# MLP down products one run later in two scan layers, and one chunk of the scan input made by another engine

## The reference

```python
def step(hst, ins):                       # one direction, over time
    dt_t, B_t, C_t, x_t = ins
    dA = jnp.exp(dt_t[:, :, None] * A)
    hst = hst * dA + (dt_t * x_t)[:, :, None] * B_t[:, None, :]
    return hst, jnp.einsum('bds,bs->bd', hst, C_t)
...
x = x + gate * (h_fwd + h_bwd)            # both directions' scans
h, gate = _adaln(x, c, adaln_mlp_w, adaln_mlp_b)
mlp_out = jax.nn.silu(h @ mlp_w1) * (h @ mlp_w2) @ mlp_w3
return x + gate * mlp_out
```

## Time and profile before

| | us |
|---|---|
| median of 3 runs | 4444.14 |
| lowest, highest | 4440.59, 4447.8 |
| the profiled execution | 4434.66 |
| its span, first to last instruction | 4432.9 |

### The profile page before, as it was taken

One profiled execution on the slowest core, in us unless ns is written; L12 is line 12 of the kernel. 1 busy time (PEld: TensorE's weight loads), 2 busy tenths in 40 slices (PEclk: granted clock), 3 DMA queues, 4 the chain that ended last, 5 costly groups with the idle time before them and its releaser, 6 DMA issues.

```text
span 4432.9 us, 109964 instructions
## 1 busy us (share of the span) xinstructions
PE 4148.3 (94%) x45790; PEld 3230.5 (73%) x45790; DVE 4007.4 (90%) x3859; ACT 3865.3 (87%) x6050; POOL 3623.7 (82%) x1328
## 2 busy tenths in 40 slices
PE   9999899899899988999989999999999999999998
PEld 6457677677677764458877777778777778777777
DVE  6669999999999976659999999999999999999996
ACT  4569899899899964569999999999999999999995
POOL 3339898798889973349999998999998999988995
PEclk9999999999999999999999999999999999999999
DMA  4012122121122221032242422422422423323221
GB/s 168 1 29 68 58 66 66 53 59 67 57 60 67 65 78 41 1 44 82 86 80 83 87 67 77 83 77 82 83 76 74 81 83 94 66 81 67 76 79 40
DMA packets 241501, 305.18 MB, mean 69 GB/s; under 512 B 116449, under 2 KB 175713, under 8 KB 241009
## 3 DMA queue, kind: packets, MB, share of 16 engines
q1 hardware_dynamic: 241008, 298.15, 24.5%
HBM read 289.84 MB, written 8.26 MB: 67 GB/s over the span
## 4 chain that ended last, share of the span: by engine, by line
PE 39%; ACT 37%; DVE 15%; issue 7%; POOL 1%; DVEq 0%; DMA 0%; SPq 0%; POOLq 0%; ACTq 0%
ACT weights_c L1800 10%; PE psum L863 9%; DVE work L2316 8%; PE psum L1152 8%; PE psum L1134 7%; ACT work L1817 7%; PE psum L1131 7%; ACT work L1800 7%; PE psum L1279 5%; ACT weights_c L1817 5%; DVE weights_c L2316 4%; ACT L1498 2%; ACT modulation L1800 2%; PE psum L1362 1%; PE psum L1075 1%
## 5 line engine op out<-in xcount | busy, mean ns | idle before, releaser
L2739 POOL TENSOR_TENSOR work<-work,weights_a 128x2048 f32<-128x2048 f32 x512 | 1977.0, 3872 | 139.9 <-DVE work L2316 106.6
L2316 DVE TENSOR_TENSOR_SCAN work<-weights_c,psum 128x512 f32<-128x512 f32 x1316 | 1509.0, 1203 | 81.0 <-PE psum L1134 69.3
L2739 POOL TENSOR_TENSOR weights_c<-weights_c,weights_a 128x2048 f32<-128x2048 f32 x256 | 989.4, 3873 | 50.2 <-DVE weights_c L2316 49.6
L1134 PE MATMUL psum<-ident,work 128*128 128x128 f32 x5464 | 932.6, 273 | 0.0
L1800 ACT ACTIVATE work<-work,decay 128x504 f32<-128x504 f32 x1172 | 817.8, 709 | 53.4 <-DVE weights_c L2316 27.4
L1134 PE MATMUL psum<-ident,weights_c 128*128 128x128 f32 x3752 | 694.5, 275 | 0.0
L2316 DVE TENSOR_TENSOR_SCAN work<-work,psum 128x512 f32<-128x512 f32 x586 | 675.2, 1201 | 20.1 <-PE psum L1134 16.9
L2316 DVE TENSOR_TENSOR_SCAN weights_c<-work,psum 128x512 f32<-128x512 f32 x586 | 675.7, 1201 | 19.1 <-PE psum L1134 18.5
L1152 PE MATMUL psum<-ident,work 64*128 64x64 f32 x16800 | 659.0, 229 | 10.6 <-POOL work L2739 7.6
L1134 PEld LDWEIGHTS psum<-ident,work 128*128 128x128 f32 x5464 | 668.2, 142 | 0.0
L1152 PEld LDWEIGHTS psum<-ident,work 64*128 64x128 f32 x16800 | 586.7, 140 | 99.8 <-issue 75.4
(11 more groups left out here) (221 smaller groups left out, 6453.9 us busy)
## 6 DMA issues: line engine op xcount, KB each, us to landing
weights_a<-c_rows SPq DMA_DIRECT2D x384, 512.0 KB, 3.7
work<-b_diagonals SPq DMA_DIRECT2D x240, 128.0 KB, 2.2
weights_c<-b_diagonals SPq DMA_DIRECT2D x112, 128.0 KB, 2.1
b_diagonals<-weights_c SPq DMA_DIRECT2D x1, 4096.0 KB, 18.1
weights_c<-in_L_cond_fwd_in_w SPq DMA_DIRECT2D x8, 512.0 KB, 5.2
weights_c<-in_L_cond_fwd_xproj_w SPq DMA_DIRECT2D x4, 1024.0 KB, 7.3
weights_c<-in_L_cond_bwd_in_w SPq DMA_DIRECT2D x8, 512.0 KB, 5.4
weights_c<-in_L_cond_bwd_xproj_w SPq DMA_DIRECT2D x4, 1024.0 KB, 7.5
```

Source lines behind the costliest of these rows:

```text
L1134: last = nc.tensor.transpose(PS[:, bank, t * P:(t + 1) * P], buf["scaled"][s % INPUTS][t][:, j * P:(j + 1) * P], IDENT[:, :])
L2316: v.tensor_tensor_scan(buf["ring"][s % RING][:, along, j], buf["decay"][q % DECAYS[l]][:, along], PS[:, 4 + q % LOOKAHEAD, along], 0.0, AL ...
L2739: g.tensor_tensor(state, state, row.unsqueeze(2).broadcast_to([P, T, DC]), ALU.mult).then_inc(ss["prod_ready"], 1)
```

## The change

It does four things.

1. Layer 3: down0 goes from runs 2, 4, 6 to the head of runs 3, 5, 7, ahead of down1. With it out of the list, the other jobs of runs 2, 4, 6 are spread wider: "dt" ends at step 205, "bc" stands at 208 to 216, "bt" at 220. In runs 3, 5, 7 down0 is at steps 3 to 11, down1 at 15 to 23, and what follows is later: the turns of "ytb" at 27 to 39 instead of 15 to 27, "in" at 115 to 139 instead of 108 to 133.
2. Layer 1: both downs of runs 3 and 5 go to runs 4 and 6, ahead of "ytb": down0 at step 3, down1 at 7 to 9. Those of run 7 and of the last block stay. The gated values (GLU1) get other memory, and the MLP norm of runs 4 and 6 waits for down1.
3. Runs 2, 4, 6 of layer 3: in every third state (`fourth_by_pool`) GpSimd scales the fourth chunk too, and TensorE turns it, where it made the diagonal product: 64 states in all, 256 products become transposes. The diagonals are still loaded.
4. In the same runs half of the thirds that were GpSimd's are ScalarE's: 32 ACTIVATEs more there, 32 operations fewer on GpSimd, which has 64 fourths more.

```diff
+def downs1(r):
+    return r // 2 - 2 if r in (4, 6) else r // 2 - 1 if r in (RUNS - 1, RUNS) else None
...
-def third_by_pool(s):
-    return s % INPUTS == 1
+def crowded(l, s):
+    return l == 3 and closes(s // PIPES[3].states)
+def third_by_pool(l, s):
+    return s % INPUTS == 1 and not (crowded(l, s) and s % (2 * INPUTS) == 1)
+def fourth_by_pool(l, s):
+    return crowded(l, s) and s % INPUTS == 0
...
     if r >= 3 and r % 2:
-        jobs += [("down1", DC, 3)]
+        jobs += [(f"down{c}", DC, 3) for c in range(KC)]
...
-    if closes(r):
-        jobs += [("down0", DC, 5)]
...
+    if tail and head and downs1(r) is not None:
+        jobs += [("down0", HIDDEN1, 3), ("down1", HIDDEN1, 3)]
     if tail:
         jobs += [(f"ytb{j}", 1, 3) for j in range(DC)] + [(f"out{c}", DC, 3) for c in range(KC)]
...
-    if gated:
+    if gated and downs1(r) is not None:
         jobs += [("down0", HIDDEN1, 3), ("down1", HIDDEN1, 8)]
...
-PIPES = {1: Pipe(32, 2, pipe_jobs1, 1, lambda r: 2 if r % 2 else 12 if r >= 2 else -IN_GAP),
+PIPES = {1: Pipe(32, 2, pipe_jobs1, 1, lambda r: 2 if r % 2 or r in (4, 6) else 12 if r >= 2 else -IN_GAP),
...
-        GLU1 = lambda r: region(WORK, 9216, HIDDEN1, T) if r < RUNS else region(WC, 13824, HIDDEN1, T)
+        GLU1 = lambda r: [A3.rearrange("p d j n -> p (d j n)"), region(SPENT, 0, T), H1B[:, 0, :]] if r < RUNS else [
+            region(WC, 13824 + T * k, T) for k in range(HIDDEN1)]
...
-            scaled=[[region(WORK, 11264 + o, DI) for o in (0, 512, 1024)],
+            scaled=[[region(WORK, 11264 + o, DI) for o in (0, 512, 1024)] + [region(SPENT, T, DI)],
...
-                    nc.tensor.matmul(PS[:, bank, SCALED * P:T], buf["dtx"][r % 2][:, SCALED, j * P:(j + 1) * P],
-                                     buf["diagonal"][:, s // 2 % 2, s % 2, :], start=True, stop=True)
-                    for t in range(SCALED):
+                    if j == 0 and fourth_by_pool(l, s):
+                        pe.wait_ge(ss["fourth_ready"], len([k for k in range(s + 1) if fourth_by_pool(l, k)]))
+                    if not fourth_by_pool(l, s):
+                        nc.tensor.matmul(PS[:, bank, SCALED * P:T], buf["dtx"][r % 2][:, SCALED, j * P:(j + 1) * P],
+                                         buf["diagonal"][:, s // 2 % 2, s % 2, :], start=True, stop=True)
+                    for t in range(TT if fourth_by_pool(l, s) else SCALED):
...
-                    loaded = n >= 2 * MADE_HERE
-                    mine_here = SCALED - 1 if third_by_pool(s) else SCALED
+                    loaded = n >= 2 * MADE_HERE or fourth_by_pool(l, s)
+                    mine_here = SCALED - 1 if third_by_pool(l, s) else SCALED
...
                     if ends:
-                        yield from tail(r, plan, bank, done, YT1(r), Z1, f"silu_z@{r - 2}", nb)
+                        yield from tail(r, plan, bank, done, YT1(r), Z1, f"silu_z@{r - 2}", nb,
+                                        close(downs1(r)) if head and downs1(r) is not None else ())
...
-                        yield from norm(r, plan, done, 3, H1B, nb, f"up2@{r - 1}" if r >= 4 else None)
+                        yield from norm(r, plan, done, 3, H1B, nb, f"down1@{r if head else r - 1}" if r >= 4 else None)
...
+                def chunks(s):
+                    if third_by_pool(l, s):
+                        chunk(s, 2, "third_ready")
+                    if fourth_by_pool(l, s):
+                        chunk(s, SCALED, "fourth_ready")
```

67 lines of the change are left out of this document (34 added, 33 removed).

## The result

The changed kernel takes 4452.75 us (median of 20 runs, 4447.55 to 4460.56), the kernel before in the same session 4443.97 (20 runs, 4436.18 to 4450.37). The ratio is 1.0023, 95% interval [1.0018, 1.0029]: the change makes the kernel 8.8 us **slower**. 4433 was forecast, and 4446 was the end of the range. The profiled execution took 4450.12 us with a span of 4448.1.

A forecast was written before the change was run, and what follows sets the result against it. The scan on VectorE was taken as the floor, with VectorE's idle time in crowded runs to win. The terms -8.5 + 1.0 - 4.5 + 1.0 = -11 against 4444.1 gave 4433 us, range 4417 to 4446.

The forecast's parts named there:

- Part 3: Layer 1, downs of runs 3 and 5 moved to runs 4 and 6: +1.0 us, bounds -5 and +7.
- They enter the head of run 4: Layer 1, receiving head: 2.4 us of VectorE work plus 1.5 of new idle, +3.9 a run.
- They leave a stretch where TensorE is busy 46.9 of 47.2: Layer 1, runs losing the downs: 2.4 us of VectorE work plus 1.0 of idle saved, -3.4 a run.
- The point that I had set for the forecast to be wrong: Layer 1, head of run 4: forecast wrong if it takes over 6 us more; other failure signs concerned layer 3.
- Part 1, the stall: Layer 3, runs 2, 4, 6: less VectorE idle around TensorE's "bc" wait, -8.5 us, bounds 0 and -12.
- no TensorE wait of over 2 us: Expected sign in layer 3: TensorE waits no more than 2 us for ScalarE's "bc" copy.
- no half clock behind it: Expected sign in layer 3: TensorE does not run at the lower clock after the "bc" wait.
- Part 1, the receiving runs: Layer 3, runs 3, 5, 7: down0's VectorE work of 1.2 us a run plus 0.3 a run, the latter booked as +1.0.
- Part 2: Layer 3, runs 2, 4, 6: transposes for diagonal products, half the thirds by ScalarE, -4.5 us, bounds 0 and -16.5.
- ScalarE's thirds: Rival: ScalarE, with 6.5 us more, bounds layer 3's runs 2, 4, 6; total -4, 4440 us; chance 0.26.
- the relief: Rival: TensorE's relief in layer 3's runs 2, 4, 6 pays in full; total -22, 4422 us; chance 0.17.
- GpSimd is no bound: Rival denied here: GpSimd becomes the bound in layer 3's runs 2, 4, 6; +22, 4466 us; chance 0.10.

The follow-up runs named there:

- e3: Kernel before with only layer 3's down0 one run later; chunks and layer 1 as before: 4434.17 us, ratio 0.9988.
- e2: Changed kernel with layer 1 put back as before, so only the layer 3 changes (down0 move and chunks): 4434.62 us, ratio 0.9986.
- e13: Layer 3 as e10, other jobs of runs 3, 5, 7 at old steps; layer 1 downs moved, residual first, other jobs at old steps, turns earlier: 4427.06 us.
- run 5: Not a follow-up kernel: a numbered stretch of a scan layer within one execution; before the change 302.2 us in layer 3, 185.7 us in layer 1.
- e4: Kernel before with only the chunk changes in layer 3's runs 2, 4, 6; down products and layer 1 as before: 4433.37 us, ratio 0.9983.
- e8: Changed kernel, layer 1: down0's VectorE operations ahead of the copies, other jobs at old steps, downs one product a step: 4436.59 us, ratio 0.9991.
- e6: Changed kernel, layer 1's runs 3 to 6: other jobs at the steps of before, downs one product a step: 4445.42 us, ratio 1.0012.
- e10: e2 with all thirds left to GpSimd, none given to ScalarE: 4428.98 us, ratio 0.9971.
- e12: e2 with down1 starting two steps later in layer 3's runs 3, 5, 7: 4433.74 us, ratio 0.9982.
- e15: Layer 3 as e10; layer 1's downs stay in runs 3 and 5, only turns bt, dtx0, dtx1 earlier: 4429.29 us, ratio 0.9955.

## Why the prediction was wrong

**Part 3: this step failed.** "They enter the head of run 4 ... I put 1.5 of new idle on it: +3.9 a run" measured +7.4 and +8.0. The mechanism was named correctly, with its place: the sums are copied only after scan 9, down0's residual stands behind them, TensorE wants the bank at step 7. Its price was not: VectorE was idle 4.0 us in the head for 0.9 before in run 4 and 0.0 in run 6, so 3.1 and 4.0 of new idle time for the 1.5 that I put there. I had priced TensorE's pause (4.6 forecast, 3.0 measured) and not what stands around it: three products due at one step, and two products at the lower clock level. And I looked no further than the head: the downs ahead of "ytb", with a start ten steps earlier, moved out0, out1 and mean by up to two steps and cost 2.1 more. "They leave a stretch where TensorE is busy 46.9 of 47.2 ... -3.4 a run" measured -1.0 and -1.8. There the freed time went to a wait that already existed behind it, 1.70 us, and grew to 3.23, and to a plan spread by 0.655 instead of 0.635 that put 20 product records into steps 64 to 79 where 16 were. My bounds for part 3 ended at +7; it cost 12.6. The point that I had set for the forecast to be wrong, a head over 6 us longer, was all but reached in run 4 (5.8) and passed in run 6 (6.9).

**Part 1, the stall: the number near, the mechanism not.** I took 8.5 us off for TensorE's wait for the "bc" copy, and with the moved 3.5 that is -12; the three MLP runs fell by 12.8 with down0 alone (e3). But only 3.0 of them stand from step 208 on, no more than down0's own operations, and VectorE is idle there 12.3 us for 12.6 (15.1 in the changed kernel). The idle time left steps 208 to 223 and came back in steps 224 to 255. The other 9.8 us come from steps 0 to 207, where I had booked nothing for down0's move but a mention that the work gets thinner. That the two nearly cancel is luck. The signs that I set say the same: "no TensorE wait of over 2 us" and "no half clock behind it" failed, with 2.12 us in run 4, 2.32 in run 6 and a granted clock of 0.91 and 0.89 in steps 224 to 239 of these runs.

**Part 1, the receiving runs: mis-sized.** Charged were 1.2 us of work and 0.3 more a run, 4.5 in all; measured 8.3 (e3), 8.7 (e2), 11.0 (the changed kernel). Of e3's 8.3 us, 7.2 stand ahead of step 208, where the jobs closer together cost more than the two operations: steps 80 to 111 of the three runs alone take 3.6 more. With the other jobs at their old steps (e13) these stretches are as before, and the cost stands in the first 32 steps. The last 16 steps differ by 2 us with the clock for the same code (run 5: 22.4 and 20.4 for 18.9).

**Part 2: the sum right, of two terms that I had not put so high.** -4.5 was forecast; e4 shows -4.3 over runs 2 to 7 in the profile and -7.5 by the ratio, [-12, -3]. It is 10.7 us won ahead of step 208, 5.8 of them in the 112 steps that I had named, less 5.7 behind it, where the wait for "bc" is longer. TensorE's saving was 9.6 us in run 4 for 9.4. The Trainium skill (FP8 and Floating Point Precision, TensorE Precision Notes) has four passes for true FP32 without exception, by which nothing would have been saved; the measurement decides against it. The rivals don't hold in full: ScalarE's thirds cost 4.2 us in the mean and not all of the part, the relief was not worth all of it, and GpSimd is no bound even with 11 more chunks. For GpSimd I had counted 16 us of side operations where my own figures leave 13.2 (282.4 less 247.3 and 21.9), so its sum is 294 and not 296; measured 292.2 in run 4.

With layer 1 as before, the rest lands at 4434.6 us (e2), where -12 on 4444.1 makes 4432. By the ratio it won 6 us, and by the profile's sums 6.9, so it fell short by 5 or 6 us; part 3's miss is the larger, 11.6.

## What to carry to other kernels

Where one PSUM bank serves all side work, a removed job is a removed buffer of time: look at which wait for another engine stands behind it before booking the gain. Where a moved job lands, check on the reading engine's own order what its release stands behind, and count the products that fall on one step. A plan that spreads jobs evenly moves all of them when one is added; run both with the other jobs pinned before judging the move, and look at what the spread had won elsewhere, which pinning gives away (2.7 us in steps 32 to 63 here). And when a stall is gone from a stretch, sum the engine's idle time to the end of the run before booking the gain: here it had moved behind the stretch.

## What the runs showed of the hardware that I had not expected

The clock after a pause. In e8 TensorE stood still for 2.92 us ahead of dtx2's turn, and the turn took 0.66 us, near the usual 0.60; the 16 steps have a granted clock of 1.00 and take 20.5 us. In e6, whose run 3 has the same jobs at the same steps, the same pause was followed by this:

```profile
954.63 1.11 PE L894 MATMUL psum<-ident,work 128*128 128x128 f32 x4 [2.92 <-ACT work L1600]
```

The turn takes 1.11 us and the 16 steps 22.1, at a granted clock of 0.92. In run 5 of e6 the same pause of 2.92 us left the clock at 1.00 (20.5 us). The kernel before shows it too: TensorE pauses for 1.43 us in the heads of runs 4 and 6 of layer 1 alike, and run 4's takes 20.6 us at a granted clock of 0.92, run 6's 19.6 at 1.00; e10, e12 and e15, with the same code there, have 19.6 in both. So 1.0 to 1.6 us hang on whether a pause of one and the same length costs the clock, and these traces don't tell what decides it.

An engine at 98% need not hold anybody up: GpSimd was busy 302.2 of 308.2 us in e10.
